# Local-attention layers with shifted inputs as values, one product matrix a head, and probabilities turned in 32x32 blocks

## The reference

```python
def attn_layer(x, Wqkv, qs, ksc, Wo):            # x already shifted: columns 64..127 come from the row before
    q, k, v = split(x @ Wqkv)                    # 16 heads of 64
    q = l2norm(q) * qs;  k = l2norm(k) * ksc
    q = q*cos*scale + rotate_half(q)*sin*scale   # k alike, with 1/scale
    sim = q_window @ [k_window_before, k_window].T * 8     # windows of 32 rows, 64 keys
    out = softmax(masked sim) @ [v_window_before, v_window]
    return out @ Wo
def ffn_layer(x, ...): layer norm, 128 -> 2 x 341, a * gelu(gate), 341 -> 128, + b2
for i in range(6):
    x = attn_layer(shift_tokens(x), ...) + x
    x = ffn_layer(shift_tokens(x), ...) + x
```

## Time and profile before

| | us |
|---|---|
| median of the runs | 2910.03 |
| the runs, lowest to highest | 2907.69 to 2917.73 (3 runs) |
| span of the profiled execution | 2911.7 |
| PE busy | 2789.5 (96%) |
| DVE busy | 2336.3 (80%) |
| ACT busy | 1746.4 (60%) |
| POOL busy | 1680.3 (58%) |

### The profile page before, as it was taken

The page is one execution under the profiler, slowest core; times in us unless marked ns, Lnnn a source line. Parts: engine busy times, 40 slices in busy tenths (PEclk is TensorE's granted clock), DMA queues, the critical chain, the costliest instruction groups (busy, mean ns, idle before and its releaser), DMA issues.

```text
span 2911.7 us, 98296 instructions
## 1 busy us (share of the span) xinstructions
PE 2789.5 (96%) x40886; PEld 1832.5 (63%) x40886; DVE 2336.3 (80%) x3830; ACT 1746.4 (60%) x2618; POOL 1680.3 (58%) x1454
## 2 busy tenths in 40 slices
PE   8999999999999999899999999999999999999997
PEld 5556565655665655566656666666666666666665
DVE  6777755774677776998968999889998999898884
ACT  4455555555666665556666666666666666666663
POOL 1000002000466665676767888878887888788882
PEclk9999999999999999999999999999999999999999
DMA  3000000000011111243234434333443343333332
GB/s 97 1 1 1 1 1 3 1 1 10 21 45 46 45 46 31 77 129 79 73 103 106 99 86 114 84 93 88 114 95 91 92 118 91 88 89 83 89 85 66
DMA packets 183114, 188.24 MB, mean 65 GB/s; under 512 B 77517, under 2 KB 130515, under 8 KB 181139
## 3 DMA queue, kind: packets, MB, share of 16 engines
q1 hardware_dynamic: 182675, 181.94, 24.8%
HBM read 61.00 MB, written 6.03 MB: 23 GB/s over the span
## 4 chain that ended last, share of the span: by engine, by line
PE 73%; DVE 10%; issue 5%; POOL 5%; SPq 3%; ACT 3%; DMA 1%; DVEq 0%; POOLq 0%; ACTq 0%
PE ps L1348 13%; PE ps L587 13%; PE ps L1356 5%; PE ps L1400 5%; PE ps L1442 4%; PE ps L1363 4%; PE ps L622 4%; PE ps L600 4%; PE ps L1389 2%; PE ps L1456 2%; PE ps L1409 2%; PE ps L534 2%; PE ps L605 2%; PE ps L1457 2%; DVE nmx L695 2%
## 5 line engine op out<-in xcount | busy, mean ns | idle before, releaser
L1348 PE MATMUL ps<-wqkv,xcT 128*128 128x512 f32 x1152 | 553.2, 603 | 4.7 <-DVE area L1886 1.6
L587 PE MATMUL ps<-xnT,qp 128*128 128x512 f32 (+3 forms) x1280 | 527.1, 543 | 17.2 <-ACT prob L814 16.3
L2030 POOL TENSOR_TENSOR ra<-ra,rb 128x1024 f32<-128x1024 f32 x191 | 452.4, 2375 | 121.9 <-DVE rb L1854 121.0
L814 ACT ACTIVATE prob<-ps,ebias,shift 128x1024 f32<-128x1024 f32 (+7 forms) x384 | 360.3, 955 | 124.0 <-DVE ebias L704 60.4
L822 ACT ACTIVATE probT<-ps 128x512 f32<-128x512 f32 (+3 forms) x384 | 207.9, 541 | 353.6 <-PE ps L600 353.5
L587 PEld LDWEIGHTS ps<-xnT,qp 128*128 128x128 f32 x1280 | 231.7, 191 | 273.6 <-issue 228.5
L2049 POOL TENSOR_TENSOR ra<-ra,rn 128x1024 f32<-128x1024 f32 x192 | 362.3, 1908 | 8.9 <-DVE ra L1946 1.2
L695 DVE TENSOR_REDUCE nmx<-ps 128x1 f32<-128x1024 f32 (+7 forms) x256 | 245.8, 987 | 108.3 <-PE ps L587 93.3
L1348 PEld LDWEIGHTS ps<-wqkv,xcT 128*128 128x128 f32 x1152 | 196.7, 190 | 154.3 <-issue 143.5
L1630 ACT ACTIVATE sq<-ps 128x1024 f32<-128x1024 f32 x192 | 195.6, 1019 | 85.6 <-PE ps L1348 85.3
L1852 DVE TENSOR_TENSOR ra<-ps,tab 128x1024 f32<-128x1024 f32 x192 | 233.6, 1217 | 3.7 <-issue 3.1
(11 more groups left out here) (274 smaller groups left out, 5651.9 us busy)
## 6 DMA issues: line engine op xcount, KB each, us to landing
vw<-vs SPq DMA_DIRECT2D x576, 130.0 KB
vw<-vs SPq DMA_DIRECT2D x384, 65.0 KB
bc<-bc_scratch SPq DMA_DIRECT2D x128, 128.0 KB, 2.9
area<-bc_scratch SPq DMA_DIRECT2D x128, 128.0 KB, 4.3
wqkv<-lwqkv_dram SPq DMA_DIRECT2D x6, 1536.0 KB, 8.6
xc<-xs SPq DMA_DIRECT2D x96, 32.0 KB
wo<-lwo_dram SPq DMA_DIRECT2D x6, 512.0 KB, 9.6
xc<-xs SPq DMA_DIRECT2D x96, 31.8 KB
```

The costliest lines, as they stand in the source:

```text
L587: mm = E.matmul(ps[:, 2 * r + o // 512, 0:w], k.qp[:, group % 2, g % NTH * P:(g % NTH + 1) * P], k.xnT[:, k0 + o:k0 + o + w], start=True, ...
L814: A.activation(k.prob[:, r, 0:nk], ps[:, 2 * r:2 * r + 2, :].rearrange("p a b -> p (a b)")[:, 0:nk], ACT.Exp, bias=k.ebias[:, row % 2:row ...
L1348: mm = E.matmul(to[:, c, :], k.xcT[:, n % 4, :], k.wqkv[l % 2][:, at + 512 * c:at + 512 * (c + 1)], start=True, stop=True)
L2030: G.tensor_tensor(k.ra[:, n % 2, w, :], k.ra[:, n % 2, w, :], k.rb[:, w, :], ALU.add).then_inc(s("added_" + what), 1)
```

## The change

**Values.** The projection of v is gone, and with it the DMAs of `spread_values` and the column of ones. Since out @ Wo summed over the heads is the sum over h of P_h x (Wv_h Wo_h), the kernel multiplies Wv and Wo of each head into one 128x128 matrix `wvo` once a layer (`fold` on PE, `folded` on ACT, two halves of 8 heads, in steps 0 and 16(l-1)+8 and +9), and applies the probabilities to the layer's shifted input itself: `mix` multiplies, for each of the four windows, 32 rows of `xc` or of `xp` (32 x 128, stationary) with 32 partitions x 512 columns of the turned probabilities. `xp` is `xc` moved by 32 rows, made by one or two DMAs a tile (`keys_before`). `side` then multiplies 16 matrices (one a head) where it had 8.

**Probabilities.** ACT takes the exponentials of all 1024 columns in one instruction. DVE sums them, takes the reciprocals, multiplies, and turns the result by one `transpose` in blocks of 32x32. PE's `turn_probs`, `values` and `turn_out` are gone, and so are DVE's copies and divisions from PSUM. ACT copies two products of `mix` (1024 columns each) into `mixT` in place of `vs` and the turned outputs.

**DVE steps.** `rotate` is one instruction of 2048 elements each for q and for k; `shift` subtracts in one instruction and not two; the squares of q and k are summed in one of 2048. POOL's `add` becomes two instructions of 512. The copy of the scan's last state goes from DVE to ACT (`state`). The bias `b2` becomes a row of `w2` met by a row of ones in `hv`, and POOL's additions of it are gone.

**Places.** The scan's units begin one step later (FIRST_UNIT 23), the taps and the small projections are spread anew, and `pair_table` is a new one.

```diff
-VALUE_HEADS = [2 * (2 * c + i) + o for i in range(2) for o in range(2) for c in range(4)]
+XRING, PRING = 8, 4
...
-TAPS = {3: 3, 4: 3, 5: 3, 6: 2, 7: 3, 8: 3, 9: 2, 10: 2, 11: 3, 12: 3, 13: 2, 14: 1}
+TAPS = {4: 3, 5: 3, 6: 3, 7: 3, 8: 3, 9: 3, 10: 2, 11: 3, 12: 3, 13: 2, 14: 2}
...
+        a, b, c, d = (2, 3, 0, 1) if n % 2 else (0, 1, 2, 3)
+        table.update({("scores", n): a, ("q", n + 2): b, ("late", n): d, ("k", n + 2): c, ("extra", n): d, ("side", n): a, ("rows_q", n + 1): b, ("rows_k", n + 1): c,
+                      ("mix0", n): a, ("mix1", n): b})
...
+    def keys_before(n):
+        b = n % PRING
+        S.wait_ge(s(f"xc{n % 2}"), 48 * (n // 2 + 1))
...
+        S.dma_start(k.xp[WIN:P, b, :], k.xc[0:P - WIN, n % XRING, :]).then_inc(s(f"xp{n % PRING}"), 16)
...
+    def fold(place, n, l, half):
+        to = pair((place, n), ("folded", 2 * l + half + 1))
+        E.wait_ge(s("wvo"), 32 * (l + 1))
+        for j in range(4):
+            for o in range(2):
+                at = slice(o * DH, (o + 1) * DH)
+                mm = E.matmul(to[:, o, j * P:(j + 1) * P], k.wvT[at, 4 * half + j, :], k.wo[at, 4 * half + j, :], start=True, stop=True, skip_group_check=True)
+        mm.then_inc(s("fold_mm"), 1)
...
+    def mix(n):
+        to = [pair((f"mix{i}", n), ("mixT", 2 * n + i + 1)) for i in range(2)]
+        E.wait_ge(s("prT"), n + 1)
+        E.wait_ge(s(f"xp{n % PRING}"), 32 * (n // PRING + 1) - (0 if n % PRING else 16))
+        prT = k.prT[:].rearrange("p (c a q) -> p c a q", a=2, q=WIN)
+        for half in range(2):
+            for w in range(4):
+                at = slice(WIN * w, WIN * (w + 1))
+                of = k.xc[at, n % XRING, :] if half == 0 else k.xp[at, n % PRING, :]
+                mm = E.matmul(to[w // 2][:, w % 2, :], of, prT[at, :, 1 - half, :], start=half == 0, stop=half == 1, skip_group_check=True)
...
-            for c in range(8):
-                mm = E.matmul(to[:, 0, 0:P], k.oT[:, c * P:(c + 1) * P], k.wo[:, l % 2, c, :], start=c == 0, stop=c == 7, skip_group_check=True)
+            for c in range(H):
+                mm = E.matmul(to[:, 0, 0:P], k.mixT[:, c, :, :].rearrange("p w q -> p (w q)"), k.wvo[:, l % 2, c, :], start=c == 0, stop=c == H - 1, skip_group_check=True)
...
+    def normalise(n):
+        pr = k.pr[:].rearrange("p (h d) -> p h d", d=DH)
+        V.wait_ge(s("exp"), n + 1)
+        V.tensor_reduce(k.suml[:], pr, X_AXIS, ALU.add).then_inc(s("v"), k.v.up())
+        V.wait_ge(s("v"), k.v.n)
+        V.reciprocal(k.recl[:], k.suml[:]).then_inc(s("v"), k.v.up())
+        V.wait_ge(s("v"), k.v.n)
+        V.tensor_tensor(pr, pr, bcast(k.recl[:], 2, DH), ALU.mult).then_inc(s("v"), k.v.up())
+        V.wait_ge(s("v"), k.v.n)
+        if n:
+            V.wait_ge(s("mixed"), 2 * n)
+        V.transpose(k.prT[:], k.pr[:]).then_inc(s("prT"), 1)
...
-        V.tensor_tensor(out_a, of, bcast(tab[:, 2 * w, :], 1, H), ALU.mult)
-        V.tensor_tensor(out_b[:, :, 0:32], of[:, :, 32:64], bcast(tab[:, 2 * w + 1, 0:32], 1, H), ALU.mult)
-        V.tensor_tensor(out_b[:, :, 32:64], of[:, :, 0:32], bcast(tab[:, 2 * w + 1, 32:64], 1, H), ALU.mult).then_inc(s("rotated_" + what), 1)
+        V.tensor_tensor(k.rot[:, n % 2, w, :, :].rearrange("p c (h d) -> p c h d", d=DH), bcast(heads(what, n), 1, 2),
+                        bcast(k.tab[:, n % FRAME, 2 * w:2 * w + 2, :], 2, H), ALU.mult).then_inc(s("rotated_" + what), 1)
...
-        G.tensor_tensor(k.ra[:, n % 2, w, :], k.ra[:, n % 2, w, :], k.rb[:, w, :], ALU.add).then_inc(s("added_" + what), 1)
+        G.tensor_tensor(a[:, :, 0:DH // 2], a[:, :, 0:DH // 2], b[:, :, DH // 2:DH], ALU.add)
+        G.tensor_tensor(a[:, :, DH // 2:DH], a[:, :, DH // 2:DH], b[:, :, 0:DH // 2], ALU.add).then_inc(s("added_" + what), 1)
```

More of the change, by code:

```diff
@@ L1530, in project_in @@
     def project_in(place, n, m):
-        to = pair((place, n), ("in_out", 2 * m + 2))
+        to = pair((place, n), ("in_out", 2 * IN_ORDER.index(m) + 2))
         for q in range(2):
@@ L1599, in transformer_pe @@
             rates(n, RATE_STEPS[n])
+        for place, l, half in FOLDS.get(n, ()):
+            if place == "late":
+                fold(place, n, l, half)
+        if n + 2 < NTILE:
+            project_k(n + 2)
+        for place, l, half in FOLDS.get(n, ()):
+            if place == "extra":
+                fold(place, n, l, half)
+        forward(n)
+        if n == HAT_STEP:
+            turn_hat()
+        if n in IN_EXTRA:
+            project_in("extra", n, IN_EXTRA[n])
+        if n <= NTILE:
+            side(n)
+        if n + 1 < NTILE:
+            turn_rows("q", n + 1)
+            turn_rows("k", n + 1)
         if n < NTILE:
-            turn_out(n)
-        if n == NTILE - 1:
-            forward(n)
+            mix(n)
 def transformer_act(k):
@@ L1758, in transformer_act @@
     for n in range(LAST_STEP):
+        if 1 <= n <= NTILE:
+            mix_out(n - 1, 0)
+            mix_out(n - 1, 1)
         if n + 2 < NTILE:
             square("q", n + 2)
+        for u in units(n):
+            if u // NS + 1 < NCH:
+                state(u)
         for u in units(n + 1):
@@ L1763, in transformer_act @@
             unit_decay(k, u)
-        if n + 3 < NTILE:
-            turned_input(n + 3)
-        if new_frame(n + 1) and n + 1 < NTILE:
-            halo_turned(n + 1)
+        if n in IN_LATE:
+            projected_in("late", n, IN_LATE[n])
+        if n == FACTOR_STEP:
+            factors(n)
+        if n in RATE_STEPS:
+            rates(n, RATE_STEPS[n])
+        for place, l, half in FOLDS.get(n, ()):
+            folded(place, n, l, half)
         if n < NTILE:
@@ L1933, in down, with scan @@
         V.wait_ge(s("down_mm"), m + 1)
-        V.tensor_tensor(k.xs[:, t + 1:t + 5, :], k.ys[:, t + 1:t + 5, :], pair("extra", 4 * m + 10)[:, 0, :].rearrange("p (t d) -> p t d", d=P), ALU.add).then_inc(s("x_down"), 1)
+        V.tensor_tensor(k.xs[:, t + 1:t + 5, :], k.ys[:, t + 1:t + 5, :], pair("extra", 4 * m + 10)[:, 0, :].rearrange("p (t d) -> p t d", d=P), ALU.add).then_inc(s("layer_x"), 1)
+    def scan(u):
+        c, i, b = u // NS, u % NS, u % 2
+        V.wait_ge(s("decay"), u + 1)
+        V.wait_ge(s("du_b"), u + 1)
+        if u >= UNITS // 2 + NS:
+            V.wait_ge(s("state"), u - NS - UNITS // 2 + 1)
+        for a in range(ET):
+            h = k.hx[:, b, a, :]
+            ins = V.tensor_tensor_scan(h, k.dc[:, b, a, :], h, k.last[:, i, a:a + 1], ALU.mult, ALU.add)
+        ins.then_inc(s("scanned"), 1)
     heads_dve(k)
@@ L1994, in transformer_dve @@
             down(m - 1)
-        elif what and what != "turn_normal" and not gate_first:
-            gated(m, int(what[2]))
         if n == NTILE + 3:
@@ L2324 @@
     qs, ks = a["L1_ffn_q_scale"], a["L1_ffn_k_scale"]
-    turned = lambda v: np.concatenate([v[:, DH // 2:], v[:, :DH // 2]], 1)
-    by_heads = lambda v, axis, order: np.concatenate([np.take(v, range(DH * h, DH * h + DH), axis) for h in order], axis)
     b1 = np.zeros((L, P, 6), np.float32)
```

351 lines of the change are left out of this document (116 added, 235 removed).

## The result

The changed kernel takes 3021.39 us (median of 5 runs, 3018.88 to 3036.54) where the kernel before took 2911.80 (5 runs): a ratio of 1.039 with a 95% interval from 1.036 to 1.042. It is slower by 4%. The prediction said 2871 with a range from 2812 to 2938, so the sign was wrong and the range didn't hold the time. The profiled execution is the slowest of the five (3036.54, 15 above the median); its span is 3034.7 us against 2911.7 for the one before. So numbers from this trace overstate the loss somewhat.

A forecast was written before the change was run, and what follows sets the result against it. PE was taken as the bound, DVE about half a microsecond behind. Gains of 31 (steps 23 to 93), 12 (early) and about 5 (end), less 10 for folds and start 1, gave 39 us: 2871 us, range 2812 to 2938.

The forecast's parts named there:

- the cover: PE's wait of 1 to 2 us ahead of `mix`, under which `down`, folds and doubled `side` cost nothing.
- forecast of 17.1 us a step: Average step in steps 23 to 93, down from 17.53, taken as a middle; 31 us gained there.
- median about 1.7: DVE's multiply by the reciprocals: shortest 1.2 us, median about 1.7, since it waits 0 to about 0.95 for POOL.
- rival (b): Port decides: multiply and POOL delay each other, scans meet POOL too; at 1.6 us of waits 2944 us; chance 0.15.
- behind POOL: Case where DVE's multiply waits for POOL's `add` and ends at 11.7 us, not 10.8; next scores at 17.4, not 16.5.
- The reading of the earlier trace: Two-SBUF-operand scans on DVE took 1.38, 2.17 or 3.30 us; the wait is about what is left of POOL's instruction.
- the prediction's account of DVE behind the transpose: `finish`, gate, squares, clamp and scans, 4.8 to 5.7 us beside PE's 4.5; up to a microsecond late costs nothing.
- The chain of an ordinary step: From scores to next scores through q, ACT's squares, `rotate`, multiply, transpose and `mix`: 16.5 us, or 17.4 meeting POOL.
- rival (c): `mix` matmuls don't run side by side on PE: about 3020 us two at a time, near 3380 singly; chance 0.07.
- The prediction's sign for ACT holding the squares back: If ACT's copies of `mix` delay the squares, DVE idles longer than 0.7 us ahead of L1831.
- Steps 0 to 22 were to gain 12 us: Eleven early steps, bound by taps on DVE, gain about nothing; the other twelve gain 1 us each.
- the value forecast for a multiply that seldom meets POOL: A rival: the multiply meets no POOL work, steps of 16.5 to 16.6 everywhere, 2830 us; chance 0.22.

The follow-up runs named there:

- late_turn: The changed kernel with `turn_normal` moved behind the turning of q and k, directly ahead of `mix`, and ACT's copy likewise: 2942.69 us, 1.012 of the kernel before.
- three: The changed kernel with the late `turn_normal`, ACT's square of k ahead of the exponentials, and ACT scaling the feed-forward input: 2848.12 us, 0.980 of the kernel before.

## Why the prediction was wrong

**The step that failed is the cover.** The prediction said: "PE waits 1 to 2 us in front of `mix`; that is the cover under which the longer step with `down`, the folds' matmuls and the doubled `side` cost nothing", and "with the steps of `down` no longer than the others". The wait in front of `mix` is real: 154.0 us in all for 96 steps, 1.6 a step. But in the step with `down` shown above it is gone (2383.72, 0.40 us). For `turn_normal` has a condition of its own, POOL's scaling, and it stood 5 us earlier in the step than before. I counted how long PE's work with `down` is (16.7 us) and not when each of its instructions may start. The rows of the order ahead of the prediction show `up` now ahead of the product (L1446, L1447, L1416, L1432), and I drew nothing from it for `turn_normal`, which has the same place in its step. The prediction weighs waits that are new; this one is old. It had cost nothing, with a margin of 0.3 us, because PE was late, and the change made PE early. No rival had it. Undoing it brought 79 us (run 1).

Sized from the table, the middle stretch missed its forecast of 17.1 us a step by 127 us: 17 steps with `down` at 4.7 us above it are 80, the 18 with n % 4 = 1 at 1.5 above are 27, and the other 36 at 0.55 above are 20.

**The multiply was mis-sized.** The forecast had it between 1.2 and 2.2 us, "median about 1.7" and above 2.3 for rival (b); it was 2.22 at the median and 2.03 in the mean. Half of the mechanism of rival (b) is there: the wait pushes POOL back too (L466). The other half isn't: the scans meet POOL less than before. I had taken the middle of my two ends. But a step of which every part repeats puts the multiply at the same place against POOL's `add` nearly every time, so the end "behind POOL" was the likely value and no average; by the mean of 2.18 us in steps 23 to 93 against 1.7, an estimated 34 us of the miss. The reading of the earlier trace rows, that the wait is what is left of POOL's instruction, holds for the common case. In three multiplies of 96 it doesn't:

```profile
2224.67 1.27 POOL L2000 TENSOR_TENSOR rot<-rot 128x512 f32<-128x512 f32 x1
...
2229.59 1.27 POOL L490 TENSOR_TENSOR acc<-acc,area 128x512 f32<-128x512 f32 x1
```

```profile
2224.25 7.69 DVE L1819 TENSOR_TENSOR area<-area,recl 128x1024 f32<-128x1024 f32 x1
```

Five instructions of POOL, these two and three between them, each of 1.27 or 1.28 us, run back to back while one multiply of DVE stands. The Trainium skill ("SBUF — State Buffer", Who interferes with whom) speaks of an exclusive lock for the whole instruction; the rows agree, and show that its holder can take it again before the one who waits.

**The step with the layer norm's statistics was overlooked.** With n % 4 = 1, DVE has the statistics (0.86 us) and their aggregation (0.38) between the clamp and the scans, as it had before; the prediction's account of DVE behind the transpose leaves them out:

```profile
2363.83 0.86 DVE L1859 BATCH_NORM_STATS2 bnst<-area 128x6 f32<-128x128 f32 x4
...
2365.03 1.36 DVE L1913 TENSOR_TENSOR_SCAN acc<-acc,last 128x256 f32<-128x256 f32 x2
2366.31 1.20 DVE L1808 TENSOR_REDUCE nmxl<-ps 128x16 f32<-128x1024 f32 x1
```

The maximum follows without a wait, so DVE is late there, with 1.2 us more to do. I had said that up to a microsecond of lateness costs nothing because the wait for the square of k absorbs it. These steps are 0.9 to 1.3 us longer than the mean of those with n % 4 = 0 and 3 in every version of the change in the table, and were 0.4 longer before, when PE was the bound.

**What was right.** The chain of an ordinary step, walked through in the prediction at 17.4 us "behind POOL", is 2404.95 - 2387.64 = 17.31 us from maximum to maximum in step 63. The parts agree: `rotate` 2.29 us for 2.29, the transpose 1.245 for 1.2, DVE's wait for the square of k there, PE's wait ahead of `mix` 1.6 for 1 to 2. `mix` takes 2402.66 - 2400.73 = 1.93 us for 2.2. So rival (c) is false, although its 3020 us is almost the measured time: one number can't tell a mechanism. The starts of the records in another step show that it does run side by side (ns min/median/max, first and last start):

```profile
L1398 PE MATMUL ps<-area,xc x8: 587/626/692, 2511.1 to 2511.7; 32*128 32x512 f32 x8
...
L1398 PE MATMUL ps<-area,xp x8: 587/587/588, 2512.0 to 2512.5; 32*128 32x512 f32 x8
```

By the Trainium skill ("TensorE: Matmul & The Clock Gate", Measured speedup vs the span model) the run would have been an estimated 2.5 us. Here the eight would take 6.9 to 7.6 us in a row (0.86 to 0.95 each, as the prediction read it) and take 1.93: a factor of 3.6 to 3.9, above that page's 3.07.

With the wait of `turn_normal` out of the way, in late_turn, the steps with n % 4 of 0 and 3 last 16.9 us in the mean, a little below the 17.1 forecast. The prediction's sign for ACT holding the squares back was idle time above 0.7 us ahead of L1831. That isn't there as a rule: 24 of 192 idle times are above it, and the median is 0.40.

**What else moved.** Steps 0 to 22 were to gain 12 us, less their part of the 10 for the folds; they lost 19, and late_turn alone brings them back to the 18.3 us a step of before. The end was to gain 5 and lost 6.

That "three" has 16.59 us a step in 23 to 93, the value forecast for a multiply that seldom meets POOL (16.5 to 16.6), is no confirmation. Its multiply still takes 1.52 us in the mean, 0.3 above the shortest, and its square of k comes earlier than in the chain that was priced; the two work against each other.

## To carry to other kernels

When a change relieves the engine that is the bound, list every wait in that engine's queue, the old ones above all, with the time at which each is satisfied and the time at which the engine will now arrive; a wait with no idle time in the trace of before may have only 0.3 us of margin. Do it for each kind of step, not for the one that the timeline happens to show. An instruction in an in-order queue whose result is needed late belongs late, ahead of the engine's next unavoidable wait; moving two calls was worth 79 us here, and having the awaited result 1 us sooner 23.
